# A cross-attention kernel on one core: a new order around the second output tile, and a last block tile by tile

## The reference

```
# layer 0
q = x @ Wq.T + bq;  k = ctx @ Wk.T + bk;  v = ctx @ Wv.T + bv
s = where(mask == 0, -1e9, q @ k.T)
x = softmax(s) @ v + x
# layer 1, 16 heads of 32 columns; the keys and values come from ctx again
Q = x @ W_qkv[:512].T + b;  K, V = ctx @ W_qkv[512:].T + b   (two thirds)
context = softmax(Q K^T / sqrt(32)) @ V          # each head
y = context @ W_o.T + b_o + x
out = (y - mean(y)) / sqrt(var(y) + 1e-5) * gamma + beta
```

## Time and profile before

| | us |
|---|---|
| timed runs, median (lowest, highest) | 436.24 (433.89, 436.6) |
| the profiled execution | 433.85 |
| its span, first to last instruction | 432.1 |
| TensorE matmul busy | 395.1 (91%) |
| VectorE busy | 273.3 (63%) |
| ScalarE busy | 281.4 (65%) |
| GpSimd busy | 222.0 (51%) |

### The profile page before, as it was taken

The page is one execution under the profiler, slowest core; times in us unless marked ns, Lnnn a source line. Parts: engine busy times, 40 slices in busy tenths (PEclk is TensorE's granted clock), DMA queues, the critical chain, the costliest instruction groups (busy, mean ns, idle before and its releaser), DMA issues.

```text
span 432.1 us, 12183 instructions
## 1 busy us (share of the span) xinstructions
PE 395.1 (91%) x4968; PEld 298.2 (69%) x4968; DVE 273.3 (63%) x679; ACT 281.4 (65%) x813; POOL 222.0 (51%) x245
## 2 busy tenths in 40 slices
PE   4999997799999999999999999999999998997960
PEld 4996755577767687777777776767776776775840
DVE  0145466467766875786668776677677866476256
ACT  0432777676688676876588558856785778667122
POOL 0400366225547843784378547755576537534353
PEclk9999999999999999999999999999999999999895
DMA  8993103400042302330053005320413012600112
GB/s 263 400 324 101 41 4 126 139 6 3 2 141 77 123 2 85 133 124 2 26 189 104 24 2 168 102 72 2 165 68 110 0 31 76 215 5 9 42 49 97
DMA packets 19230, 39.44 MB, mean 91 GB/s; under 512 B 1865, under 2 KB 5449, under 8 KB 18151
## 3 DMA queue, kind: packets, MB, share of 16 engines
q1 hardware_dynamic: 18599, 37.72, 25.8%
q10 hardware_dynamic: 576, 0.96, 0.7%
HBM read 26.49 MB, written 8.39 MB: 81 GB/s over the span
## 4 chain that ended last, share of the span: by engine, by line
PE 75%; DVE 12%; ACT 5%; DMA 4%; issue 1%; SPq 1%; POOL 0%; DVEq 0%
PE ps_q L864 19%; PE ps_out L929 17%; PE ps_t L889 11%; PE ps_s L878 7%; PE ps_pv L904 7%; PE ps_out L825 4%; PE ps_s L801 4%; PE ps_s L944 2%; ACT prob L475 2%; DVE mx L655 2%; DMA p_b<-p_l 2%; DVE m L573 2%; DVE sm L662 1%; ACT pt L484 1%; DMA raw<-in_w0k 1%
## 5 line engine op out<-in xcount | busy, mean ns | idle before, releaser
L339 POOL TENSOR_TENSOR prob<-prob,rc 128x308 f32<-128x308 f32 x128 | 91.9, 725 | 158.8 <-DVE rc L664 157.6
L475 ACT ACTIVATE prob<-ps_s,mx 128x77 f32<-128x77 f32 x512 | 121.2, 328 | 0.7 <-DVE mx L655 0.7
L484 ACT ACTIVATE pt<-ps_t 77x512 f32<-77x512 f32 x128 | 76.3, 596 | 57.6 <-PE ps_t L889 57.0
L655 DVE TENSOR_REDUCE mx<-ps_s 128x4 f32<-128x308 f32 x128 | 54.8, 471 | 46.8 <-PE ps_s L878 46.8
L889 PE MATMUL ps_t<-ident,prob 128*77 128x128 f32 x512 | 79.8, 279 | 3.9 <-ACT pt L484 3.3
L662 DVE TENSOR_REDUCE sm<-prob 128x4 f32<-128x308 f32 x128 | 59.6, 466 | 35.0 <-ACT prob L475 34.9
L889 PEld LDWEIGHTS ps_t<-ident,prob 128*77 128x77 f32 x512 | 61.8, 148 | 23.7 <-issue 8.7
L864 PE MATMUL ps_q<-x_h,wq_h 128*128 128x512 f32 x128 | 53.4, 417 | 0.0
L864 PE MATMUL ps_q<-x_h,wq_l 128*128 128x512 f32 x128 | 53.0, 414 | 0.0
L318 POOL TENSOR_TENSOR x_l<-x_raw,x_h 128x512 fp32r<-128x512 f32 x32 | 41.2, 1292 | 21.2 <-ACT x_h L428 21.2
L929 PE MATMUL ps_out<-wo_h,ct_h 128*128 128x512 f32 x112 | 46.3, 413 | 0.0
(11 more groups left out here) (111 smaller groups left out, 608.5 us busy)
## 6 DMA issues: line engine op xcount, KB each, us to landing
x_raw<-in_xT SPq DMA_DIRECT2D x8, 1024.0 KB, 6.5
y<-in_x SPq DMA_DIRECT2D x28, 256.0 KB, 2.8
out<-y SPq DMA_DIRECT2D x28, 256.0 KB, 2.0
p_b<-p_a SPq DMA_DIRECT2D x8, 154.0 KB
mask_sb<-in_mask SPq DMA_DIRECT2D x7, 154.0 KB, 5.4
raw<-in_w0k SPq DMA_DIRECT2D x2, 512.0 KB, 6.8
raw<-in_w0q SPq DMA_DIRECT2D x2, 512.0 KB, 10.0
raw<-in_w0v SPq DMA_DIRECT2D x1, 1024.0 KB, 12.2
```

Of the source, the lines that this page charges most:

```text
L339: nc.gpsimd.tensor_tensor(ap, ap, wide(rc[:, k % 2, h], KEYS), ALU.mult).then_inc(prob_done, 1)
L475: e = nc.scalar.activation(prob[:, k % 2, h, t], ps_s[:, h, t * KEYS:(t + 1) * KEYS], ACT.Exp, bias=mx[:, k % 2, h, t:t + 1])
L484: nc.scalar.activation(pt[:, h], ps_t[0:KEYS, :], ACT.Copy).then_inc(pt_ready, 1)
L655: nc.vector.reduce_max(mx[:, k % 2, h], ps_s[:, h, 0:TILES * KEYS].rearrange("p (t k) -> p t k", k=KEYS), AX_X, negate=True).then_inc(max_ ...
```

## The change

Three things. In the steps g = 1 and 2 the query's last four matmuls come before part(1) of the output; VectorE adds tile 0's residual ahead of layer 0's shift and the sums of head 2; and at g = 3 the output's 14 matmuls are cut 4, 5, 5 in place of 5, 3, 6. For the last unit TensorE gets a list of its own (`last_step`): transposes of its four heads with short groups of output matmuls between them, its context, then what is left, tile by tile; ScalarE splits its context ahead of two normalisations of the block before. For the last block the norm is done by tile: bn_aggr takes mean and variance, GpSimd takes each tile's root, ScalarE normalises tiles 0 and 1 and GpSimd does their gamma and beta, and VectorE does tiles 2 and 3 in two operations each: (y - mean) * gamma, then times the root plus beta. Tiles are stored in the order 0, 2, 3, 1.

```
-OUT_AT = {1: (0, 14, 18, 22), 2: (22, 28, 36, 42), 3: (42, 47, 50, 56)}
+OUT_AT = {1: (0, 14, 18, 22), 2: (22, 28, 36, 42), 3: (42, 46, 51, 56)}
...
# SyncE
-            for t, (semaphore, count) in enumerate(((beta_done, TILES * LAST + 1), (last_beta_done, 1),
-                                                    (last_beta_done, 2), (last_beta_done, 3))):
+            for t, semaphore, count in ((0, beta_done, TILES * LAST + 1), (2, last_beta_done, 1),
+                                        (3, last_beta_done, 2), (1, beta_done, TILES * LAST + 2)):
...
# GpSimd, behind the steps
-            root(0, LAST, 0)
-            root(0, LAST, 1)
...
+            last_root(0)
+            last_root(1)
+            last_gamma(0)
+            last_root(2)
+            last_beta(0)
+            last_root(3)
+            last_gamma(1)
+            last_beta(1)
...
# ScalarE, step
-                round_ct(i, k - 2)
+                if k <= UNITS:
+                    round_ct(i, k - 2)
...
+                    if k == UNITS:
+                        round_ct(i, k - 1)
                     if g == 0:
                         normalise(i, b - 2, 2)
...
             run(act, step)
-            for t in range(TILES):
-                normalise(0, LAST, t)
+            for t in range(2):
+                act.wait_ge(last_nb_done, t + 1)
+                nc.scalar.activation(last_y[:, t], last_y[:, t], ACT.Identity, bias=last_nb[:, t:t + 1],
+                                     scale=last_rs[:, t:t + 1]).then_inc(z_done, 1)
...
# VectorE, step
                 inverse_sums(i, k, 1)
+                if g == 1 and b <= LAST:
+                    residual(i, b - 1, 0)
                 if g == 1:
                     layer0_shift(i, b + 1)
...
                 inverse_sums(i, k, 2)
-                if g == 1 and b <= LAST:
-                    residual(i, b - 1, 0)
...
+            def last_moments(t):
+
+                dve.wait_ge(bn_done, TILES * LAST + t + 1)
+                nc.vector.bn_aggr(last_mv[:, t], bn6[:, t]).then_inc(last_mv_done, 1)
+                dve.wait_ge(last_mv_done, t + 1)
+                nc.vector.tensor_scalar(last_ve[:, t:t + 1], last_mv[:, t, 1:2], LN_EPS, None, ALU.add).then_inc(last_ve_done, 1)
+
+            def last_offset(t):
+
+                dve.wait_ge(last_rs_done, t + 1)
+                nc.vector.scalar_tensor_tensor(out=last_nb[:, t:t + 1], in0=last_mv[:, t, 0:1], scalar=-1.0,
+                                               in1=last_rs[:, t:t + 1], op0=ALU.mult, op1=ALU.mult).then_inc(last_nb_done, 1)
+
+            def last_gamma(t):
+
+                nc.vector.scalar_tensor_tensor(out=last_y[:, t], in0=last_y[:, t], scalar=last_mv[:, t, 0:1],
+                                               in1=rows_sb[:, 0], op0=ALU.subtract, op1=ALU.mult).then_inc(last_gamma_done, 1)
+
+            def last_beta(t, n):
+
+                dve.wait_ge(last_rs_done, t + 1)
                 dve.wait_ge(last_gamma_done, n + 1)
-                nc.vector.tensor_tensor(last_y[:, t], last_y[:, t], rows_sb[:, 1], ALU.add).then_inc(last_beta_done, 1)
+                nc.vector.scalar_tensor_tensor(out=last_y[:, t], in0=last_y[:, t], scalar=last_rs[:, t:t + 1],
+                                               in1=rows_sb[:, 1], op0=ALU.mult, op1=ALU.add).then_inc(last_beta_done, 1)
 
             run(dve, step)
             residual(0, LAST, 0)
+            statistics(0, LAST, 0)
+            last_moments(0)
             residual(0, LAST, 1)
-            statistics(0, LAST, 0)
+            last_offset(0)
             statistics(0, LAST, 1)
-            variance(0, LAST, 0)
+            last_moments(1)
             residual(0, LAST, 2)
+            last_offset(1)
+            statistics(0, LAST, 2)
+            last_moments(2)
+            last_gamma(2)
             residual(0, LAST, 3)
-            statistics(0, LAST, 2)
-            offset(0, LAST, 0)
             statistics(0, LAST, 3)
-            variance(0, LAST, 1)
-            offset(0, LAST, 1)
-            last_affine(1, 0)
-            last_affine(2, 1)
-            last_affine(3, 2)
+            last_moments(3)
+            last_beta(2, 0)
+            last_gamma(3)
+            last_beta(3, 1)
...
# TensorE; last_output(t, first, last) now issues matmuls first to last - 1 of tile t's 14
+            def last_step():
+
+                transposes(0, UNITS - 1, 0)
+                last_output(0, 0, 2)
+                last_output(1, 0, 2)
+                transposes(0, UNITS - 1, 1)
+                last_output(2, 0, 2)
+                last_output(3, 0, 2)
+                transposes(0, UNITS - 1, 2)
+                last_output(0, 2, 6)
+                transposes(0, UNITS - 1, 3)
+                last_output(0, 6, 10)
+                context(0, UNITS - 1)
+                last_output(0, 10, 11)
+                last_output(1, 2, 11)
+                last_output(0, 11, OUTPUT)
+                last_output(1, 11, OUTPUT)
+                last_output(2, 2, OUTPUT)
+                last_output(3, 2, OUTPUT)
...
                 else:
+                    query(i, k + 1, 10, QUERY)
                     part(1)
-                    query(i, k + 1, 10, QUERY)
                     part(2)
                 context(i, k - 1)
...
-            run(pe, step)
-            last_output(3, CH)
+            for k in range(UNITS):
+                step(0, k)
+            last_step()
```

More of the change, by code:

```diff
@@ L125, in xattn_kernel @@
         nb = sb("nb", [P, TILES])
+        last_mv = sb("last_mv", [P, TILES, 2])
+        last_ve = sb("last_ve", [P, TILES])
+        last_rs = sb("last_rs", [P, TILES])
+        last_nb = sb("last_nb", [P, TILES])
         ps_q = ctx.enter_context(nc.psum_tensor("ps_q", [P, 512], F32))
@@ L395, in _, with last_root, last_beta @@
             run(pool, step)
-            root(0, LAST, 0)
-            root(0, LAST, 1)
-            m = TILES * LAST
-            pool.wait_ge(z_done, m + 1)
-            nc.gpsimd.tensor_tensor(last_y[:, 0], last_y[:, 0], rows_sb[:, 0], ALU.mult).then_inc(gamma_done, 1)
-            pool.wait_ge(gamma_done, m + 1)
-            nc.gpsimd.tensor_tensor(last_y[:, 0], last_y[:, 0], rows_sb[:, 1], ALU.add).then_inc(beta_done, 1)
+            def last_root(t):
+                pool.wait_ge(last_ve_done, t + 1)
+                nc.gpsimd.tensor_tensor(last_rs[:, t:t + 1], last_ve[:, t:t + 1], minus_half[:, 0:1], ALU.pow).then_inc(last_rs_done, 1)
+            def last_gamma(t):
+                pool.wait_ge(z_done, TILES * LAST + t + 1)
+                nc.gpsimd.tensor_tensor(last_y[:, t], last_y[:, t], rows_sb[:, 0], ALU.mult).then_inc(gamma_done, 1)
+            def last_beta(t):
+                pool.wait_ge(gamma_done, TILES * LAST + t + 1)
+                nc.gpsimd.tensor_tensor(last_y[:, t], last_y[:, t], rows_sb[:, 1], ALU.add).then_inc(beta_done, 1)
+            last_root(0)
[6 more added lines that the diff above has]
+            last_beta(1)
         @block.scalar
@@ L931, in output, with last_output @@
                         mm.then_inc(out_done, 1)
-            def last_output(first, last, tiles_of=range(TILES)):
-                wait(pe, ctl_ready, CH * LAST + last)
-                for t in tiles_of:
-                    own = slice(t * P, (t + 1) * P)
-                    if first == 0:
-                        wait(pe, exp_done, GROUP_HEADS * UNITS)
-                        for m, (w, v) in enumerate(stacked_values(LAST, own)):
-                            nc.tensor.matmul(last_out[t][:], w, v, start=(m == 0), stop=False)
-                    for c in range(first, last):
-                        for m, (w, v) in enumerate(part3(ct_h[:, LAST % 2, c, own], ct_l[:, LAST % 2, c, own], wo_h[:, c], wo_l[:, c])):
-                            mm = nc.tensor.matmul(last_out[t][:], w, v, start=False, stop=(c == CH - 1 and m == 2))
-                    if last == CH:
-                        mm.then_inc(out_done, 1)
+            def last_output(t, first, last):
+                own = slice(t * P, (t + 1) * P)
+                if first == 0:
+                    wait(pe, exp_done, GROUP_HEADS * (UNITS - 1) + t + 1)
+                else:
+                    wait(pe, ctl_ready, CH * LAST + (last - 3) // 3 + 1)
+                for m in range(first, last):
+                    if m < 2:
+                        w, v = stacked_values(LAST, own)[m]
+                    else:
+                        c = (m - 2) // 3
+                        w, v = part3(ct_h[:, LAST % 2, c, own], ct_l[:, LAST % 2, c, own], wo_h[:, c], wo_l[:, c])[(m - 2) % 3]
+                    mm = nc.tensor.matmul(last_out[t][:], w, v, start=(m == 0), stop=(m == OUTPUT - 1))
+                if last == OUTPUT:
+                    mm.then_inc(out_done, 1)
@@ L1006, in step @@
                 transposes(i, k - 1, 0)
-                if type(i) is int and k == UNITS:
-                    last_output(0, 3, [0])
                 if g == 3:
@@ L1013, in step @@
```

(13 more changed lines are left out.)

5 lines of the change are left out of this document (2 added, 3 removed).

## The result

The changed kernel takes 423.42 us, the median of 4 runs (422.43 to 424.65), beside 435.06 (433.89 to 436.6) for the kernel before in its 4 runs: 0.9745 of its time, 95% interval 0.9703 to 0.9786. The forecast was 423.0.

The account below looks back on a forecast made before the run. Bound: TensorE plus one residual wait in blocks 2 to 6, then the last unit and norm tail. Terms 5.2 + 0.2 + 7.0 = 12.4 us gave 421.4 (profiled execution) or 423.8 (median); forecast 423.0 us, range 419.5 to 427.5.

Parts of the forecast that it names:

- The sum: Whole change: 5.2 + 0.2 + 7.0 = 12.4 us saved; 421.4 from the profiled execution, 423.8 from the median.
- low end: Fast end of the range, 419.5 us: bounds of the norm (8.4) and the cuts added, 14 us from 433.9.
- Part 3: New output cuts at g = 3: 0.1 us a block, bounds -0.2 and +0.26; 0.2 us in the sum.
- Part 1: Query matmuls before part(1) at g = 1 remove TensorE's residual wait in blocks 2 to 6: 5.2 us.
- rival C: Steady steps: only the idle 3.0 us come back, not the refills; 10.2 us won, 426.0 us; 9% chance.
- Part 5: Norm tile by tile in the tail: end at 422.5 against 429.54, 7.0 us saved including TensorE's 4.3, bounds 6.0 and 8.4.
- Part 2: VectorE's earlier residual of tile 0: gives the query reorder its margin, itself worth 0, bounds -0.2 to +0.2.
- Part 4: Last unit's order: context at 403.2 against 411.49, last matmul at 413.4 against 417.71, TensorE ends 4.3 us sooner.
- A: Tail: VectorE and GpSimd hold each other up, norm stretch stays 11.4 us; 9.7 us won, 426.5 us; 12% chance.
- B: Something else is as late at g = 1, steps stay at 13.2 us; 7.2 us won, 429.0 us; 7% chance.
- D: Pauses from 397.5 on lower TensorE's clock to the last matmul: 437.5 us, 2% chance; short fall 425.0 us, 8%.
- GpSimd as the last engine by more than 1 us: Tail sign of a wrong forecast: GpSimd, with six operations queued at the end, replaces VectorE as last by over 1 us.

Follow-up runs that it names:

- b4: Kernel before with all three steady-state edits (query first, residual first, cuts 4, 5, 5) and the old tail: ratio 0.9891, 4.7 us.
- b1: Changed kernel with the old output cuts at g = 3 put back: 424.92 us, ratio 0.9778.
- a2: Kernel before with only VectorE's residual of tile 0 moved ahead of the shift and sums: ratio 0.9921, 3.4 us.
- a4: Kernel before with only the last unit's new order on TensorE and ScalarE, norm still in pairs of tiles: ratio 0.9856.
- c1: Changed kernel with tile 0's root early and tile 1's gamma and beta as two fused VectorE operations: 422.37 us, ratio 0.9747.
- a3: Changed kernel with all three steady-state edits put back, so only the new tail: ratio 0.9852, 6.4 us.
- a1: Kernel before with only the query's last four matmuls moved ahead of part(1) at g = 1 and 2: ratio 0.9924, 3.3 us.
- c0: Changed kernel itself, unchanged, run again beside c1: 425.38 us, ratio 0.9811.

## Why the prediction was right, step by step

**The sum.** 12.4 us were forecast against the profiled execution; the profile has 9.2 and the medians 11.6. The time of 423.0 fell within 0.5 us of the median, and some of that is luck. It was set between a sum from 433.85 and one from 436.24, and the median before came to 435.06; and two falls of the clock and the stand in block 4, about 2.7 us in the profiled execution, were in no term. In the low end part 3's bound of 0.26 us a block was added only once; for five blocks that end would lie near 419.0.

**Part 1, 5.2 us.** The wait went, in all five blocks. The steps gave 4.6 us in this trace (3.5 to 4.6 in the nine), and 0.8 came back as the stand in block 4; alone, the steady edits are worth 4.7 us (b4, 3.3 to 6.1 by its interval). The term of the sum that was mis-sized is "13.29 - 12.18 = 1.1 us" taken for all five: the steps of blocks 4 and 5 stood at 12.82 and 13.10 before. Pricing the wait by whole steps rather than by its idle time was right all the same: the 3.0 us of rival C would have left steps of 12.5 us, and in the nine traces they are 12.2 to 12.4 in the mean. The mask product was named as what made VectorE late; that its length goes with GpSimd's operation beside it, as in the hold-up that part 5 reckons with, wasn't seen.

**Part 2, "worth 0".** True beside part 1 and false as a price: alone it is worth as much as part 1 alone (3.4 and 3.3 us). What it adds to part 1 is 0.3 us in the steps in the mean, within their scatter. The step said that it gives part 1 its margin; which of the two is called free was a choice.

**Part 3, 0.2 us.** Nothing (b1). What the prediction gave as its own reason against, that a DMA behind transpose0 takes back what is won, would be enough; no run tests that reason.

**Part 4, 4.3 us.** 4.24 in the trace: context at T0 + 5.83 where 5.8 was said, last matmul + 15.99 where 16.0 was said, ScalarE's work of block 6 from + 7.46 where 7.5 was said and GpSimd's from + 8.34 where 8.4 was said. But the 20.23 us it was taken from held a fall of the clock of 1.6 us, which the prediction had seen and not priced; a2 and b4 run that order without it in 18.65. At full clock the order gives 2.7 us on TensorE; the rest comes only where the old order's wait lowers the clock.

**Part 5, 2.7 us** (7.0 less 4.3). 3.1 in the trace. The queues came out nearly as worked: a stand at the first offset of 1.58 us (1.2 said), bn_aggr 0.18 us (0.2 taken), last operation at T0 + 24.76 (25.1 said). Not all of the new VectorE operations read two SBUF tensors, as the prediction has it: bn_aggr (L798) and the addition behind it read one. The cause was put in the wrong place: 1.8 of it come from tiles that end one after another, which is part 4's doing, and 1.3 from the norm's new operations (a4).

**The rivals.** A fell: VectorE did wait at the offset and both engines did block each other, but six operations at the end were too few to fill 11.4 us; the stretch is 8.37. B fell, with steps of 12.2. C fell by the steps, 61.07 us where it would have left 62.6. D fell: from T0 to the last matmul the clock is 1.00 through all the short pauses. But one of the prediction's own signs of being wrong came true: GpSimd as the last engine by more than 1 us. Its last operation ends at 420.36 and VectorE's at 419.24, 1.12 us apart. The time held all the same: the 422.5 of part 5 had already reckoned with most of the two engines' work one after the other; c1 shows what giving GpSimd that work cost.

## What to carry to other kernels

Price a wait by the difference of whole steps, and look for a second edit that would remove the same wait before adding the two. At a tail where a norm runs on two engines that lock each other out, count operations that overlap, not operations per engine: moving one tile's work from the slower one to fused operations on the faster one won about 1.9 us in the trace (2.2 with the early root) though the faster one was the busier. Look for the same hold-up in the steady state: the mask product took three times as long (1.43 us for 0.48) wherever GpSimd had just begun a full operation. And before a part of the tail is credited to an order, read the granted clock in the stretch that it is compared with.

## What was not expected of the hardware

**Supply of instructions.** The stand of 0.8 to 1.6 us within layer 0's matmuls comes where TensorE waits less elsewhere: block 4's step takes 9.22 us in a4 and 9.55 and 9.56 in a3 and before, which all still have the wait for the residual and no stand, and 10.3 to 11.1 in the ten kernels without that wait whose stream isn't shifted by half a transfer. A sixth (after) to over a third (a1, a2) of what the steady edits win in the steps goes back here. The transfers' times fit this. In a4, a3 and before the transfer in question begins 1.2 to 1.3 us ahead of block 4's first layer 0 matmul, in the ten others 0.5 to 1.0 us behind it. Why it begins when it does stays open.

**The granted clock.** Ahead of block 7's step g = 1 TensorE idles 0.77 and then 0.97 us (before 359.91 and 361.94 in the profile after) in all 14 profiles. In 10 of them the clock of that step then has a mean of 0.87 to 0.88 and the step takes 13.5 to 13.8 us; in 4 (before, a4, c0, c1) it takes 12.2. In the profile after, matmuls stand 0.43 to 0.57 us apart behind it, at the lower of TensorE's two clock levels (1.2 and 2.4 GHz):

```profile
363.91 0.77 PE L912 MATMUL ps_q<-x_h,wq_h 128*128 128x512 f32 x1
364.48 0.63 PE L912 MATMUL ps_q<-x_h,wq_l 128*128 128x512 f32 x1
364.91 0.63 PE L912 MATMUL ps_q<-x_h,wq_h 128*128 128x512 f32 x1
```

c0 is the same kernel and has block 7's step at full clock: this is 1.4 us between executions of one kernel, not the change's. Block 0's step g = 3 is alike: behind a wait of 1.05 us its mean is 0.85 or 0.86 in 5 of the 14 (after and c0 among them) and 1.00 in the others. Why one execution falls and the next doesn't stays open.
